# The start of the first group in a fused attention and mixture-of-experts kernel: experts behind the gate product, combine weights spread by TensorE, attention three steps later, zeros on TensorE until xn

## The reference

```python
xn = layernorm(x)
# attention, window of 64
h = relu(xn @ nm_w1 + nm_b1);  m = h @ nm_w2 + nm_b2
q, k, v = m @ q_w + q_b, m @ k_w + k_b, m @ v_w + v_b
weights = softmax(q . k_band / sqrt(128))       # positions -32..+32 inside the sequence
attn = weights . v_band
# experts: 16, of which the top 8 count, and a shared one
scores = sigmoid(xn @ gate_w.T)
inds = top_k(scores + expert_bias, 8)
combine = onehot(inds) * scores[inds] / sum(scores[inds]) * 2.826
y = sum_e combine[e] * (silu(xn @ w_gate[e].T) * (xn @ w_up[e].T)) @ w_down[e].T
y += (silu(xn @ shared_gate.T) * (xn @ shared_up.T)) @ shared_down.T
out = x + attn + y
```

## Time and profile before

| | us |
|---|---|
| median of 3 runs (722.91 to 723.25) | 722.94 |
| the profiled execution | 722.1 |
| its span | 720.2 |
| TensorE busy | 701.5 (97%) |
| DVE busy | 574.2 (80%) |
| ACT busy | 438.9 (61%) |
| POOL busy | 399.7 (55%) |

### The profile page before, as it was taken

One profiled execution on the slowest core, in us unless ns is written; L12 is line 12 of the kernel. 1 busy time (PEld: TensorE's weight loads), 2 busy tenths in 40 slices (PEclk: granted clock), 3 DMA queues, 4 the chain that ended last, 5 costly groups with the idle time before them and its releaser, 6 DMA issues.

```text
span 720.2 us, 10617 instructions
## 1 busy us (share of the span) xinstructions
PE 701.5 (97%) x3384; PEld 577.2 (80%) x3384; DVE 574.2 (80%) x1605; ACT 438.9 (61%) x874; POOL 399.7 (55%) x356
## 2 busy tenths in 40 slices
PE   5889999999999999999999999999999999999997
PEld 4667888888888888888888888888888888888886
DVE  4788788787888878788887888878787887878775
ACT  3575665666656575665766656566655766656573
POOL 3745555546565555565556655555565555655463
PEclk9999999999999999999999999999999999999999
DMA  7704316061250615216061340615215061430600
GB/s 256 256 10 152 130 26 226 29 235 45 90 191 2 234 45 177 103 47 218 16 235 45 109 172 4 236 42 204 76 51 227 4 236 45 130 135 7 244 1 15
DMA packets 36647, 84.72 MB, mean 118 GB/s; under 512 B 7152, under 2 KB 15472, under 8 KB 36592
## 3 DMA queue, kind: packets, MB, share of 16 engines
q1 hardware_dynamic: 36592, 84.05, 33.2%
HBM read 79.32 MB, written 4.72 MB: 117 GB/s over the span
## 4 chain that ended last, share of the span: by engine, by line
PE 93%; DVE 3%; DMA 2%; ACT 1%; issue 0%; POOL 0%; SPq 0%; DVEq 0%
PE ps_y L390 26%; PE ps_u L380 26%; PE ps_g L370 26%; PE bank L348 3%; PE bank L306 3%; PE bank L329 3%; PE bank L318 2%; PE bank L311 2%; PE bank L338 2%; PE ps_y L357 1%; DMA comb_b<-c_dram 1%; DVE ps_u L889 0%; DVE h_lo L895 0%; DVE exp_w_lo L644 0%; DMA xin<-x 0%
## 5 line engine op out<-in xcount | busy, mean ns | idle before, releaser
L969 POOL TENSOR_TENSOR silu_c<-silu,comb_b 128x512 f32<-128x512 f32 x256 | 330.5, 1294 | 300.7 <-ACT silu L564 297.1
L572 ACT ACTIVATE h_hi<-ps_u 128x512 fp32r<-128x512 f32 x272 | 162.5, 598 | 261.7 <-DVE ps_u L889 259.8
L895 DVE TENSOR_TENSOR h_lo<-ps_u,h_hi 128x512 fp32r<-128x512 f32 x272 | 185.7, 683 | 59.9 <-ACT h_hi L572 59.7
L889 DVE TENSOR_TENSOR ps_u<-silu_c,ps_u 128x512 f32<-128x512 f32 x256 | 176.6, 690 | 44.5 <-PE ps_u L380 38.2
L564 ACT ACTIVATE silu<-ps_g 128x512 f32<-128x512 f32 x272 | 161.4, 594 | 0.2
L380 PE MATMUL ps_u<-xn_hi,exp_w_hi 128*128 128x512 f32 x272 | 110.7, 407 | 5.1 <-DVE h_lo L895 5.1
L390 PE MATMUL ps_y<-h_hi,exp_w_hi 128*128 128x512 f32 x272 | 112.7, 414 | 0.4 <-DVE h_lo L895 0.4
L370 PE MATMUL ps_g<-xn_hi,exp_w_hi 128*128 128x512 f32 x272 | 108.3, 398 | 0.0
L370 PE MATMUL ps_g<-xn_lo,exp_w_hi 128*128 128x512 f32 x272 | 108.0, 397 | 0.0
L370 PE MATMUL ps_g<-xn_hi,exp_w_lo 128*128 128x512 f32 x272 | 107.6, 395 | 0.0
L380 PE MATMUL ps_u<-xn_lo,exp_w_hi 128*128 128x512 f32 x272 | 107.5, 395 | 0.0
(11 more groups left out here) (139 smaller groups left out, 982.0 us busy)
## 6 DMA issues: line engine op xcount, KB each, us to landing
comb_b<-c_dram SPq DMA_DIRECT2D x64, 1024.0 KB, 8.7
xin<-x SPq DMA_DIRECT2D x16, 256.0 KB, 3.1
xres<-x_t SPq DMA_DIRECT2D x16, 256.0 KB, 2.7
out_t<-xres SPq DMA_DIRECT2D x16, 256.0 KB, 2.0
exp_raw<-wexp SPq DMA_DIRECT2D x3, 960.0 KB, 9.3
c_dram<-comb_t SPq DMA_DIRECT2D x64, 8.0 KB, 1.8
exp_raw<-wexp SPq DMA_DIRECT2D x1, 384.0 KB, 5.4
att_raw<-watt SPq DMA_DIRECT2D x1, 330.5 KB, 3.4
```

Of the source, the lines that this page charges most:

```text
L572: A(h_t[hbuf(par, s)][0][:], ps_u[(par + s) % 2][:], ACT.Copy).then_inc(s_h_hi, 1)
L889: V.tensor_tensor(ps_u[i][:], src[:], ps_u[i][:], ALU.mult).then_inc(s_h, 1)
L895: V.tensor_tensor(t[1][:], ps_u[(par + s) % 2][:], t[0][:].bitcast(F32), ALU.subtract)\
L969: G.tensor_tensor(silu_c[i][:].rearrange("p (l x) -> p l x", l=2), silu[i][:].rearrange("p (l x) -> p l x", l=2), comb_b[:, :, s1 - 1, :], ...
```

## The change

The change touches the prologues and group 0 alone, plus one wait count on the chunks of `comb_b`. `when(g, s, fresh)` gives the slot `fresh` in group 0 and s in all others.

- TensorE starts with 12 products of 512 columns on a tile of zeros (`spin`, `SPIN` = 12) that DVE clears first. The transposes of xn follow, each waiting for its own tile of xn; the merged value weights now come behind them.
- Behind the gate product come the side products (now into a bank of the up products), and then slot 0. The hidden product stands inside slot 0, the score weights in slot 1, `hid_turn` and `q_proj` in slot 3.
- The combine weights of the first four experts of group 0 are spread by TensorE: per expert four transposes of one column of `comb`, repeated, into bank 1 or 2, in slots 1 and 2, and one pass of ACT into `comb_b`. SP's first chunk for group 0 is left out. POOL waits for `s_fresh` for these experts.
- The attention of group 0 stands about three slots later (scores in slots 5 and 7, xn of group 1 in slot 5, its gate product in slot 7, transposed probabilities in slots 10 and 12); the attention products stay in slots 13 and 14.
- The experts' weights come in transfers of 1, 2, 4, 5 and 5; the expert bias and x of group 1 are issued later. POOL makes lo of all but experts 6 and 8, four of them ahead of slot 0 and the rest in its slots.
- A bias vector is scaled by DVE before the side product and not after it, and the three copies out of the side products are one.

```diff
-EXPW = [(0, 2), (2, 7), (7, 12), (12, STEPS)]
+EXPW = [(0, 1), (1, 3), (3, 7), (7, 12), (12, STEPS)]
-EARLY = 8
+DVE_LO = (6, 8)
+SPIN = 12
 # SP
                 store_comb(0, 0)
-                for c in range(NCHUNK):
+                for c in range(1, NCHUNK):
                     spread(0, 0, c, True)
 # TensorE
+            def spin(times):
+                for _ in range(times):
+                    mm(ps_u[1][:], spin_in[:, 0:P], spin_in[:], start=True, stop=True)
+            def fresh_weights(e, dst):
+                for a in range(TILES):
+                    done = nc.tensor.transpose(dst[:, a * P:(a + 1) * P],
+                                               comb[:, a, e:e + 1].to_broadcast([P, P]), ident[:])
+                done.then_inc(s_fresh_mm, 1)
+            def fresh_att(s):
+                if s == 1:
+                    pe.wait_ge(S["comb"], 1)
+                    fresh_weights(0, bank[1])
+                    pe.wait_ge(s_attw, 1)
+                    fresh_weights(1, bank[2])
+                    score_weights()
+                if s == 2:
+                    pe.wait_ge(s_fresh, 1)
+                    fresh_weights(2, bank[1])
+                    pe.wait_ge(s_fresh, 2)
+                    fresh_weights(3, bank[2])
+                if s == 3:
+                    hid_turn(0)
+                    pe.wait_ge(s_scw, 1)
+                    pe.wait_ge(s_row, 1)
+                    pe.wait_ge(s_fresh, 3)
+                    q_proj(0)
             def prologue():
+                pe.wait_ge(s_spin, 1)
+                spin(SPIN)
+                pe.wait_ge(s_const, 1)
+                for a in range(TILES):
+                    if a < TILES - 1:
+                        pe.wait_ge(s_xn_tile, a + 1)
+                    else:
+                        pe.wait_ge(S["xn"], 1)
+                    done = nc.tensor.transpose(bank[1][:, a * P:(a + 1) * P], xn[:, a, :], ident[:])
...
             def slot(g, par, s):
                 if first(g) and s == 0:
                     gate_proj(g, par, s)
+                    pe.wait_ge(s_attw, 1)
+                    hid_proj(0, 0)
 # ACT
+            def fresh_weights(e, src):
+                act.wait_ge(s_fresh_mm, e + 1)
+                A(comb_b[:, :, e, :], src[:].rearrange("p (l x) -> p l x", l=2), ACT.Copy).then_inc(s_fresh, 1)
+            def fresh_att(s):
+                if s == 0:
+                    expw_hi(3)
+                if s == 1:
+                    fresh_weights(1, bank[2])
+                    score_weights()
+                    expw_hi(5)
+                    hid_relu(0)
+                if s == 2:
+                    fresh_weights(2, bank[1])
+                    fresh_weights(3, bank[2])
+                    expw_hi(6)
+                if s == 3:
+                    q_hi(0)
+                    hid_n_hi(0)
+                    expw_hi(7)
...
 # DVE
             def prologue():
+                V.memset(spin_in[:].bitcast(F32), 0.0).then_inc(s_spin, 1)
...
+            def fresh_att(s):
+                if s == 1:
+                    moments(1, 1)
+                    score_weights()
+                    variance(1)
+                if s == 2:
+                    hid_lo(0)
+                if s == 3:
+                    expw_lo(6)
+                if s == 4:
+                    q_lo(0)
+                if s == 6:
+                    expw_lo(8)
 # POOL
                 inverse_std(0)
-                for s in range(EARLY):
+                for s in range(4):
                     expw_lo(s)
-                inverse_std(1)
             def slot(g, par, s):
+                if first(g) and s in (1, 2):
+                    expw_lo(s + 3)
+                if first(g) and s == 2:
+                    inverse_std(1)
+                if first(g) and 6 <= s <= 13:
+                    expw_lo(s + 3)
                 if s1 > 0:
...
-                    if (s1 - 1) % CHUNK == 0:
-                        pool.wait_ge(s_comb_b[(s1 - 1) // CHUNK], 16 * g1 + 16)
+                    if first(g1) and s1 <= CHUNK:
+                        pool.wait_ge(s_fresh, s1)
+                    elif (s1 - 1) % CHUNK == 0:
+                        c = (s1 - 1) // CHUNK
+                        pool.wait_ge(s_comb_b[c], 16 * (g1 + (c > 0)))
...
+                if first(g) and s == 4:
+                    expw_lo(7)
```

More of the change, by code:

```diff
@@ L211, in first, with when @@
             return g == 0
+        def when(g, s, fresh):
+            return fresh if first(g) else s
         def last(g, ahead=0):
@@ L362, in gate_proj @@
                 if first(g):
-                    if s < EARLY:
-                        pe.wait_ge(s_expw, s + 1)
+                    late = sum(e <= s for e in DVE_LO)
+                    if s in DVE_LO:
+                        pe.wait_ge(s_expw_late, late)
                     else:
-                        pe.wait_ge(s_expw_late, s + 1 - EARLY)
+                        pe.wait_ge(s_expw, s + 1 - late)
                 if not first(g) or s >= 2:
@@ L455, in att_early @@
                     turn(bank[1], flat(xn)).then_inc(S["xn_tp"], 1)
-                if s == 3:
-                    if not first(g):
+                if s == when(g, 3, 5):
+                    if first(g):
+                        pe.wait_ge(s_fresh, CHUNK)
+                    else:
                         pe.wait_ge(S["z_lo"], g)
@@ L460, in att_early @@
                     scores(0)
-                if s == 4 and more:
+                if s == when(g, 4, 7) and more:
                     pe.wait_ge(S["xn_lo"], g + 2)
@@ L466, in att_early @@
                     gate(1 - par)
-                if s == 5:
+                if s == when(g, 5, 7):
                     scores(1)
@@ L591, in prologue @@
                 A(key_row[:], ps_y[:, M_B:M_B + P], ACT.Copy).then_inc(s_row, 1)
-                for s in range(2, 5):
-                    expw_hi(s)
-                expw_hi(5)
-                q_hi(0)
-                for s in range(6, EARLY):
-                    expw_hi(s)
+            def fresh_weights(e, src):
[18 more added lines that the diff above has]
+                if s == 4:
+                    expw_hi(8)
+                if s == 5:
+                    expw_hi(9)
+                    expw_hi(10)
+                if s == 6:
+                    expw_hi(11)
+                if s == 7:
+                    expw_hi(12)
+                if 9 <= s <= 12:
+                    expw_hi(s + 4)
             def att(g, par, s):
                 more = not last(g)
-                if first(g) and s + EARLY < STEPS:
-                    expw_hi(s + EARLY)
-                if s == 0:
+                if first(g):
+                    fresh_att(s)
+                elif s == 0:
                     hid_n_hi(g)
-                if s == 1 and more:
+                if s == when(g, 1, 5) and more:
                     xn_hi(g + 1, 1 - par)
-                if s == 5:
+                if s == when(g, 5, 8):
                     if more:
@@ L624, in slot @@
                     gate_silu(g, par, s)
+                    act.wait_ge(s_side_mm, 1)
+                    A(chain[:, 1, :], ps_u[1][:, M_B:M_B + P], ACT.Copy).then_inc(s_side, 1)
                 else:
                     h_hi(*before(g, par, s))
-                if s == 6:
+                if s == when(g, 6, 9):
                     prob_exp(g, 1)
+                if first(g) and s == 1:
+                    fresh_weights(0, bank[1])
+                    expw_hi(4)
                 if not (last(g) and s == STEPS - 1):
@@ L665, in normalise @@
                                            rstd[:, a:a + 1], ALU.subtract, ALU.mult)
+                    if first(g) and a < TILES - 1:
+                        done.then_inc(s_xn_tile, 1)
                 done.then_inc(S["xn"], 1)
@@ L765, in prologue @@
                 normalise(0, 0)
+                xn_lo(0, 0)
                 dve.wait_ge(s_attw_hi, 1)
```

131 lines of the change are left out of this document (67 added, 64 removed).

## The result

The changed kernel takes 715.63 us (median of 4 runs, 715.54 to 715.79), the kernel before 723.10 beside it: a ratio of 0.9895, with a 95% interval of 0.9877 to 0.9912. The profiled execution took 715.54 us, its span is 713.4. The forecast was 712.5 in a range of 710.0 to 717.0: the direction and the range hold, but of 10.4 us forecast 7.5 came.

What follows compares the result with a forecast made beforehand. TensorE, busy 97% of the span, was taken as the bound, idle mostly in the first 50 us. An 11.6 us earlier first attention product, less allowances of 0.9 and 0.3, left 10.4: 712.5 us, range 710.0 to 717.0.

Steps and rivals of the forecast that it cites:

- the layout: Predicted timeline of group 0 from trace durations: first attention product at 50.15 instead of 61.76, 11.6 us earlier before allowances.
- the 1.2 us of allowances: Group 0, outside the timeline: 0.9 us for TensorE's restarts and 0.3 us for VectorE remainders slowed beside POOL.
- the allowance for VectorE beside POOL: Group 0: VectorE remainders running beside POOL take longer, up to 1.34 us instead of 0.54; 0.3 us allowed.
- the rival low until step 1: TensorE's clock stays low until step 1, so step 0 starts at 13.2: gain 6.5 us, 716.4 us; chance 0.22.
- POOL is the bound: Steps 6 to 13: remainders meeting VectorE instructions and late silu products add 2.5 us: gain 7.9, 715.0 us; chance 0.18.
- The head start is handed back: Steps 1 to 5: ScalarE falls behind with roundings and spreads, losing 8 us: gain about 2.5, 720.4 us; chance 0.05.
- the wait of 0.9 us: Within steps 6 to 13: TensorE waits about 0.9 us for expert 11, whose remainder POOL makes.

Runs made afterwards that it cites:

- held_thin: held, with POOL making the remainders of experts 12 to 16 for only 8 of 384 columns, the rest zero (work left out): 713.56 us.
- h_lo_first_1: Changed kernel with score-weight copies and the variance of group 1 moved behind h_lo 0 on VectorE in slot 1: 715.76 us.
- before_zeros: Kernel before the change, with only the cleared tile and 12 zero products added at TensorE's start: 721.62 us against 722.86.
- held: Changed kernel with more zero products on TensorE: 14 ahead of the transposes, two before and two behind the gate product: 714.98 us.
- by_dram: Changed kernel with the first four experts' combine weights sent through DRAM again, without TensorE's transposes and ScalarE's passes: 723.03 us against 722.86 before the change.
- held_split: held, with the remainders of experts 10, 12, 14 and 16 made by VectorE instead of POOL: 715.76 us.
- order2: held plus VectorE work behind h_lo in four slots; group 1's variance and its power on POOL moved later, expert 7's remainder earlier: 716.39 us.
- no_zeros: Changed kernel without its 12 zero products: 717.93 us.

## Why the prediction was right, and where it was off

**The frame held.** The gain is made before the first attention product of group 0 and kept from there on: 6.8 us there, 6.8 in the span. The zeros cover TensorE's wait for xn. Step 0 was forecast at 11.25 and came at 10.93, xn_lo ended at 9.0 (forecast 9.3), comb at 14.7 (14.3). The chunks that still come by DRAM are never waited for. The wait before up 2 was 1.55 us (1.4), the one for comb_b 2 was 0.32 (0.5). The waits in steps 6 to 13 are 2.5 us, within the 3 us given.

**Where the missing 3.6 us went.** From the start of step 0 to the first attention product the layout had 38.9 us (11.25 to 50.15); it took 44.0 (10.93 to 54.93), 5.1 more. Less the 1.2 us of allowances and the 0.3 us by which step 0 was early, that is the 3.6 us between a gain of 10.4 and one of 6.8. TensorE's waits were 5.0 us where the layout had 3.6; the starts at the lower clock took 1.6 us more; and each of the five waits cost, by my estimate, 0.26 us beyond its idle time, 1.3 in all (before up 4 the start moved by 0.74 us for 0.58 of idle time, and the next start came 0.33 us later, not 0.23). Some 0.8 us stay open.

**The first term that was mis-sized is the allowance for VectorE beside POOL.** The prediction had the row (1.34 us beside 0.54) and took 0.3 us for all of group 0, as if it were a few remainders. It applies to VectorE's TENSOR_SCALAR instructions and to those with both inputs in SBUF, and the change keeps POOL busy in just those slots. From the trace after: variance 1.0 us too long, xn of group 1 1.1, the pairs of prob_n 1.05 and 0.96, the select and the weight of the routing 0.7 and 0.4. That is 5 us on VectorE, in the queue ahead of h_lo. On TensorE less arrives: its four waits for h_lo are 4.65 us, of which the layout had 1.8. In the layout up 4 stood at 26.0 and came at 28.3; step 10 ended at 43.65 and came at 46.0. held_thin shows one piece of it, 1.4 us, by experiment; the sum for all of group 0 wasn't measured by itself.

**The second is the clock.** The forecast had it high from step 0 on, the rival low until step 1. It did neither: it rose during the zeros (twelve took 4.47 us, not 5.2; in h_lo_first_1 and before_zeros they took 5.35, so the moment differs between executions), fell at about 11.4 and rose again at 14.8. The prediction had itself noted that narrow work had never raised the level, and did not ask whether such work keeps it. What held gets back of it is 0.65 us.

**The rival "POOL is the bound"** gave 715.0, within 0.6 of the result, but for a reason that is only half right; that its number lies nearer than the forecast's is in part luck. It counted a collision of 0.25 to 0.3 us in each of eight steps, and POOL's own lateness. In the changed kernel POOL waits 1.59 us for silu 10 and 1.84 for silu 13, and the only remainder that holds TensorE in steps 6 to 13 is that of expert 7, by 0.13 us, where the layout had 1.3 us of such waits. POOL was early; it was VectorE that paid.

**"The head start is handed back"** happened in part: of 10.6 us at step 0, 3.8 are gone at 55 us. ScalarE, which that rival named, has a small share. Its copies of the score weights ended at 19.10 (18.45 in the layout), VectorE waited 2.10 us for them, and the stretched variance and h_lo 0 stood behind. In by_dram, where the variance took 0.17 us and ScalarE had no spreads to make, the wait before up 2 was 1.55 us all the same.

**What was worth more than I thought** is the spread by TensorE: undone, it costs 7.4 us, the whole gain. The later slots of the attention were not tried by themselves, so what that part is worth stays open.

One sum is off by itself: 712.5 less both allowances and the wait of 0.9 us is 710.4, not the 710.0 of the range.

The Trainium skill, GPSIMD Engine Reference, Engine selection, would have had the remainders on VectorE. held_split gave four back and gained nothing (0.1 to 0.8 us slower). For one instruction the rows agree (1.00 against 0.57 us); here VectorE was the engine that came last.

## What to carry to other kernels

Price an engine's work not only by its own queue, but also by what it does to its neighbour. The first trace can show it: an instruction that takes 1.25 us at one place and 0.18 at another is such a sign. Where VectorE's small instructions run beside a busy POOL, count up to a whole POOL instruction for each, above all for those queued ahead of what TensorE waits for. When a prologue is shortened, look for the last thing that the first real step needs: here an early start was worth nothing until the combine weights came early too. And a wait that is removed, or a clock that is held, pays only as far as the next engine lets it: 1.6 us of faster products, less 0.3 for the zeros that held the clock, gave 0.65.

## What the runs showed of the hardware that I had not expected

- A VectorE TENSOR_SCALAR on 4 columns took 1.15 us beside a POOL instruction and 0.17 alone; four on 128 columns took 1.10 to 2.83 us, by how many POOL instructions they met (3.07 in by_dram). Instructions that read PSUM, such as h_lo, kept their 0.68 us.
- The clock can fall while TensorE is hardly idle. In the changed kernel it fell at about 11.4 us, after transposes, small and one-column products from 6.64 to 10.93 with no gap over 0.4 us; with two more wide zero products ahead of that time and four in it, it stayed up (held). It also stayed up there in by_dram, with the changed kernel's twelve.
- How much of a wait it bears is not fixed: after 2.68 us it stayed up in the kernel before, after 2.08 us it stayed in held and fell in held_thin, after 2.07 us it fell in held_split and after 2.25 us in order2.
- Products of zeros raise the clock too: with them the transposes and narrow products up to 10.93 us ran at the upper level, without them (no_zeros) the same took until 12.99. Transposes with one column repeated 128 times cost what transposes of xn do, eight in 1.04 us and four in 0.60.
